# An expert layer's key products over two experts at once, with matching blocks kept, and one output product per half-tiled slot tile

## What is computed

```python
x = conv_attention(x)                 # q, k, v by 1x1 convolutions, softmax over rows of the image
t = tokens(x)                         # (4, 1024, 256)
t = t + mix(layer_norm(t))            # h W1 + (band h) W2 + bias
t = t + experts(layer_norm(t))

# experts: 32 of them, each with keys 256 x 64 and values 64 x 256
sel = sigmoid(xt @ expert_sel.T)      # (4096, 32)
sel_val, sel_idx = top_k(sel, 2)      # each token goes to two experts, weighted
h = relu(einsum('td,edh->teh', xt, keys))
out = einsum('teh,te,ehv->tv', h, w, values)   # w: zero but for the two chosen
```

## Time and profile before

| | |
|---|---|
| median of 3 runs | 510.26 us (509.55 to 510.54) |
| the profiled execution | 509.37 us |
| its span, first to last instruction | 507.6 us |
| granted TensorE clock, mean | 0.878 |
| instructions | 10650 |

### The profile page before, as it was taken

The page is one execution under the profiler, slowest core; times in us unless marked ns, Lnnn a source line. Parts: engine busy times, 40 slices in busy tenths (PEclk is TensorE's granted clock), DMA queues, the critical chain, the costliest instruction groups (busy, mean ns, idle before and its releaser), DMA issues.

```text
span 507.6 us, 10650 instructions
## 1 busy us (share of the span) xinstructions
PE 399.3 (79%) x3207; PEld 292.9 (58%) x3207; DVE 362.7 (71%) x1080; ACT 229.5 (45%) x604; POOL 321.6 (63%) x479
## 2 busy tenths in 40 slices
PE   8899999999999999999999885748676277766000
PEld 4677777877778877777676662336454154534000
DVE  3778999999999999999999667546454454556100
ACT  2214454544555454545454343339655556735000
POOL 5345558888778888688888777144555554636610
PEclk9899999999999999999999976879877768767555
DMA  8996001411111111121110012575554443431096
GB/s 202 330 213 182 11 23 54 126 53 44 53 33 47 49 54 44 44 52 45 54 52 35 22 63 74 134 234 156 164 153 133 124 135 109 123 95 50 3 206 125
DMA packets 28441, 49.55 MB, mean 98 GB/s; under 512 B 6204, under 2 KB 21966, under 8 KB 27373
## 3 DMA queue, kind: packets, MB, share of 16 engines
q1 hardware_dynamic: 20512, 26.69, 20.6%
q0 software_dynamic: 7872, 22.19, 14.1%
HBM read 30.74 MB, written 25.73 MB: 111 GB/s over the span
## 4 chain that ended last, share of the span: by engine, by line
PE 51%; issue 14%; DVE 13%; SPq 9%; POOL 3%; DMA 2%; another core or an unknown queue 1%; ACT 1%; DVEq 0%; POOLq 0%; ACTq 0%
PE bank L1189 17%; SPq L396 8%; PE bank L1129 6%; PE bank L1070 6%; PE E L1094 5%; PE bank L1243 3%; PE bank L1049 2%; PE E L1229 2%; PE bank L1162 2%; PE bank L1257 2%; DVE gmax L744 2%; POOL out L568 2%; PE bank L1170 2%; DVE gsum L792 2%; PE bank L1149 2%
## 5 line engine op out<-in xcount | busy, mean ns | idle before, releaser
L568 POOL DMA_INDIRECT out<-vT,dest x80 | 78.8, 985 | 68.7 <-DVE vT L1003 47.9
L1189 PE MATMUL bank<-vT,prob 128*128 128x256 f32 x512 | 118.8, 385 | 0.0
L1189 PEld LDWEIGHTS bank<-vT,prob 128*128 128x128 f32 x512 | 95.7, 191 | 12.2
L490 POOL TENSOR_TENSOR prob<-prob,ginv 128x1024 f32<-128x1024 f32 x32 | 61.0, 1907 | 28.1 <-DVE ginv L807 25.6
L472 POOL DMA_INDIRECT slot_rows<-rows,slot x64 | 68.4, 1069 | 12.7 <-issue 12.7
L990 DVE TENSOR_SCALAR q_s<-bank 128x256 f32<-128x256 f32 x20 | 8.5, 424 | 63.1 <-remote 56.1
L1257 PE MATMUL bank<-rows,q_s 64*64 64x256 f32 (+1 forms) x224 | 36.2, 479 | 19.2 <-DVE q_s L990 10.8
L665 ACT ACTIVATE prob<-E 128x512 f32<-128x512 f32 x40 | 22.7, 593 | 55.2 <-PE E L1229 34.5
L628 ACT ACTIVATE prob<-prob 128x1024 f32<-128x1024 f32 x32 | 33.8, 1057 | 20.8 <-DVE prob L748 20.8
L1243 PE MATMUL bank<-prob,k_s 128*64 128x64 f32 (+1 forms) x448 | 32.1, 297 | 13.9 <-issue 13.2
L1229 PE MATMUL E<-ident,xc_or_xin 128*128 128x128 f32 x160 | 28.9, 336 | 16.7 <-DMA xc_or_xin<-slot_rows 15.6
(11 more groups left out here) (200 smaller groups left out, 856.7 us busy)
## 6 DMA issues: line engine op xcount, KB each, us to landing
xc_or_xin<-slot_rows SPq DMA_DIRECT2D x48, 130.0 KB
xc_or_xin<-slot_rows SPq DMA_DIRECT2D x64, 65.0 KB
xt<-x_tok SPq DMA_DIRECT2D x32, 128.0 KB, 2.4
values_s<-values SPq DMA_DIRECT2D x2, 2048.0 KB, 28.3
out<-out POOLq DMA_DIRECT2D x4, 1024.0 KB, 14.1
xc_or_xin<-x_cm SPq DMA_DIRECT2D x3, 1024.0 KB, 20.3
keys_s<-keys SPq DMA_DIRECT2D x1, 2048.0 KB, 14.2
out<-vT,dest POOLq DMA_INDIRECT x80
```

The costliest lines, as they stand in the source:

```text
L490: g.tensor_tensor(prob[:, t % 2], prob[:, t % 2], ginv[:, t % 2].unsqueeze(2).to_broadcast([P, WT * KB, W]), ALU.mult).then_inc(prob_done, 1)
L568: g.indirect_dma_start(out=out, out_offset=bass.IndirectOffsetOnAxis(ap=dest[:, n % (2 * NB), k:k + 1], axis=0), in_=yb[:, n % NB, k, :], ...
L1189: mm = m.matmul(av_p, pr[:, j, :], vT[:, b % 2, j, :], start=(j == 0), stop=(j == KB - 1))
```

## The change

It changes the shapes of three products in the expert stage and what goes with them.

- Whole tiles, hidden: the keys of two tiles' experts stand side by side as 128 columns (`kk_two`), and one product takes them against the tokens of both tiles (256 columns). Of its result the blocks where keys and tokens belong together are kept (`H_two[side, :, r, :]`), the other two are not read. 4 products (8 records) of 128 columns with 256 token columns in place of 8 (16 records) of 64 with 128.
- Half tiles, hidden: the same with the two experts of one tile (`kk_half`): 8 products (16 records) of 128 columns with 128 token columns in place of 16 (32 records) of 64 with 64.
- Half tiles, outputs: the relu's results are put on the diagonal blocks of a buffer `hT_half` whose other blocks hold zeros, so one product of 128 x 128 with 256 columns does a tile: 4 (8 records) in place of 8 (16 records).
- The relu is two instructions, one for each half of the partitions, in every group; TensorE waits for both.
- GpSimd fills the zero blocks of `hT_half` (in a part of `t2` that is free by then) by two instructions behind the last scatter of token rows, and TensorE waits for them once, ahead of the first outputs of half tiles.
- Keys and values are copied in the same number of instructions of the same size to other places.

```diff
@@ GpSimd, behind the scatters of token rows
+            pool.wait_ge(u2_copied, 2 * GROUP * P // C)
+            for r in range(2):
+                g.memset(hT_half[r * HID:(r + 1) * HID, :, :, (1 - r) * HALF:(2 - r) * HALF], 0.0).then_inc(zeroed, 1)
@@ ScalarE, keys_copied
-                        done = a.activation(kk[:, n % 2, k, r], keys_s[:, :, bass.ds(expert[2 * k + r], 1), :].rearrange(
+                        into = kk_two[:, n % 2, k // 2] if parts(n) == 1 else kk_half[:, n % 2, k]
+                        done = a.activation(into[:, :, side_of(k if parts(n) == 1 else r)], keys_s[:, :, bass.ds(expert[2 * k + r], 1), :].rearrange(
@@ VectorE, hidden
-                v.tensor_scalar(hT[:, n % 2], H_p[n % 2], 0.0, None, ALU.max).then_inc(hid_out, 1)
+                for r in range(2):
+                    side = side_of(r)
+                    if parts(n) == 1:
+                        v.tensor_scalar(hT[side, n % 2], H_two[n % 2][side, :, r, :], 0.0, None, ALU.max).then_inc(hid_out, 1)
+                    else:
+                        tokens = slice(r * HALF, (r + 1) * HALF)
+                        v.tensor_scalar(hT_half[side, n % 2, :, tokens], H_half[n % 2][side, :, tokens], 0.0, None,
+                                        ALU.max).then_inc(hid_out, 1)
@@ TensorE, hidden
-                width = P // parts(n)
-                for two in range(GROUP // 2):
-                    for r in range(parts(n)):
-                        tokens = slice(r * width, (r + 1) * width)
+                if parts(n) == 1:
+                    for two in range(GROUP // 2):
+                        pair = slice(2 * two, 2 * two + 2)
                         for a in range(CH):
-                            for k in (2 * two, 2 * two + 1):
-                                mm = m.matmul(H_p[n % 2][side_of(k), two, tokens], kk[:, n % 2, k, r, a, :],
-                                              uT[:, n % 2, k, a, tokens], start=(a == 0), stop=(a == CH - 1))
+                            mm = m.matmul(H_two[n % 2][:, two], kk_two[:, n % 2, two, a, :], uT[:, n % 2, pair, a, :],
+                                          start=(a == 0), stop=(a == CH - 1))
+                else:
+                    for k in range(GROUP):
+                        for a in range(CH):
+                            mm = m.matmul(H_half[n % 2][:, k], kk_half[:, n % 2, k, a, :], uT[:, n % 2, k, a, :],
+                                          start=(a == 0), stop=(a == CH - 1))
@@ TensorE, outputs
-                width = P // parts(n)
-                for two in range(GROUP // 2):
-                    for r in range(parts(n)):
-                        tokens = slice(r * width, (r + 1) * width)
-                        for k in (2 * two, 2 * two + 1):
-                            mm = m.matmul(Y_p[n % 2][k % 2][tokens, two, :], hT[side_of(k), n % 2, two, tokens],
-                                          vv[side_of(k), n % 2, two, r, :], start=True, stop=True)
+                if n == WHOLE_GROUPS:
+                    pe.wait_ge(zeroed, 2)
+                for k in range(GROUP):
+                    h, w = ((hT[side_of(k), n % 2, k // 2], vv[side_of(k), n % 2, k // 2, 0, :]) if parts(n) == 1
+                            else (hT_half[:, n % 2, k], vv_half[:, n % 2, k, :]))
+                    mm = m.matmul(Y_p[n % 2][k % 2][:, k // 2, :], h, w, start=True, stop=True)
```

More of the change, by code:

```diff
@@ L193, in attention_moe @@
         uT = prob.rearrange("p b j v -> p b (j v)").rearrange("p b (k a n) -> p b k a n", k=GROUP, a=CH)
-        kk = k_s.rearrange("p b g j v -> p b (g j v)").rearrange("p b (k r a n) -> p b k r a n", k=GROUP, r=2, a=CH)
+        kk = k_s.rearrange("p b g j v -> p b (g j v)")
+        kk_two = kk[:, :, 0:GROUP * CH * HID].rearrange("p b (w a n) -> p b w a n", w=GROUP // 2, a=CH)
+        kk_half = kk.rearrange("p b (k a n) -> p b k a n", k=GROUP, a=CH)
         hT = q_s[:, 0].rearrange("p t w h -> p (t w h)").rearrange("p (b k n) -> p b k n", b=2, k=GROUP // 2)
@@ L198, in attention_moe @@
             "p (b k r n) -> p b k r n", b=2, k=GROUP // 2, r=2)
+        hT_half = t2[:, 0:2 * GROUP * P // C].rearrange("p t n -> p (t n)").rearrange("p (b k n) -> p b k n", b=2, k=GROUP)
+        vv_half = vv.rearrange("p b k r n -> p (b k r) n").rearrange("p (b k) n -> p b k n", k=GROUP)
         yb = vT[:, :, :, :].rearrange("p a (b k) n -> p (a b) k n", k=GROUP)
@@ L220, in attention_moe @@
         T_p = [E[:, q * 512:(q + 1) * 512].rearrange("p (k a n) -> p k a n", k=2, a=CH) for q in range(2)]
-        H_p = [bank[2 + b][:, 0:2 * P].rearrange("p (k n) -> p k n", k=GROUP // 2) for b in range(2)]
+        H_two = [bank[2 + b][:, :].rearrange("p (w k n) -> p w k n", w=GROUP // 2, k=2) for b in range(2)]
+        H_half = [bank[2 + b][:, :].rearrange("p (k n) -> p k n", k=GROUP) for b in range(2)]
         Y_p = [[bank[i + side][:, :].rearrange("p (k n) -> p k n", k=GROUP // 2) for side in range(2)] for i in (6, 4)]
@@ L251, in attention_moe @@
         coef_done, rebuilt = sem("coef_done"), sem("rebuilt")
+        zeroed = sem("zeroed")
         cols_out, T_mm, T_out, H_mm, hid_out = sem("cols_out"), sem("T_mm"), sem("T_out"), sem("H_mm"), sem("hid_out")
@@ L1014, in values_copied @@
                     for r in range(parts(n)):
-                        done = v.tensor_copy(vv[side_of(k), n % 2, k // 2, r, :],
-                                             values_s[side_of(k), bass.ds(expert[2 * k + r], 1), :].rearrange(
-                                                 "p e n -> p (e n)"))
+                        side = side_of(k if parts(n) == 1 else r)
+                        into = vv[side, n % 2, k // 2, 0, :] if parts(n) == 1 else vv_half[side, n % 2, k, :]
+                        done = v.tensor_copy(into, values_s[side, bass.ds(expert[2 * k + r], 1), :].rearrange("p e n -> p (e n)"))
                 done.then_inc(values_out, 1)
@@ L1235, in hidden @@
                 if n >= 2:
[L1236 to L1244 removed]
+                    pe.wait_ge(hid_out, 2 * (n - 1))
+                if parts(n) == 1:
+                    for two in range(GROUP // 2):
+                        pair = slice(2 * two, 2 * two + 2)
+                        for a in range(CH):
+                            mm = m.matmul(H_two[n % 2][:, two], kk_two[:, n % 2, two, a, :], uT[:, n % 2, pair, a, :],
[5 more added lines that the diff above has]
+                                          start=(a == 0), stop=(a == CH - 1))
                 mm.then_inc(H_mm, 1)
             def outputs(n):
[L1248 removed]
+                pe.wait_ge(hid_out, 2 * n + 2)
                 pe.wait_ge(values_out, n + 1)
```

## The result

The changed kernel takes 504.21 us (median of 20 runs), the kernel before 508.56 us beside it (20 runs): a ratio of 0.9919, 95% interval 0.9895 to 0.9943, so 0.8% faster. The profiled execution of the changed kernel has a span of 503.6 us, against 507.6 before.

A forecast was written before the change was run, and what follows sets the result against it. It took the expert stage as a loop from release to release, held by scattered rows in flight. Relu 14 x 0.38 = 5.3 us, all else 0, on 509.37 gives 514.7, plus 0.9 for the median: 515.6; range 505 to 527.

The forecast's parts named there:

- The relu: VectorE's L990 split in two: 0.38 us more in each of 14 bursts, 5.3 us (4.8 to 6.4).
- The products' own time: TensorE's hidden products and half-tile outputs take longer: 12 x 0.83 + 8 x 1.6 = 23 us at full clock.
- The products' price of 0: TensorE's added work lies in the 8 to 13 us between releases, where it stands still 5 us: costed at nothing.
- the reading of a release: Expert stage: while scattered rows are in flight, TensorE's reports arrive late or not; the last row's landing releases everything.
- The prediction's 1.47: Expert stage: the release comes 1.47 us after the eighth scatter of a burst ends, part of the 13.42 us cycle.
- Rival B: Expert stage: TensorE's crawl of one instruction each 0.7 us sets the release, so fewer matmuls shorten it: 504; chance 0.17.
- TensorE drains at a change of shape: On TensorE, each change of shape costs 0.1 to 0.15 us; 36 fewer save 5 us; part of B and C.
- Rival A: TensorE late in half-tile groups, or whole-tile bursts of eight split: 11 to 13 us on top, 527; chance 0.23.
- Rival C: Expert stage: the loop waits for SyncE's loads, not the scatters; relu costs nothing, no change, 510.5; chance 0.14.

The follow-up runs named there:

- relu2: The kernel before with only the relu split into two instructions of 64 partitions: 512.03 us, ratio 1.0068 to the kernel before.
- wide_many: The changed kernel with its products cut in two, giving the matmul counts of before at the new width: 513.36 us, ratio 1.0122 to the kernel before.
- tiny_again: The changed kernel with eight one-column matmuls ahead of the hidden products of every whole-tile group, on a third chip: 512.42 us, ratio 1.0029 to the kernel before.
- no_rows: The kernel before with scatters issued but a bound that drops nearly all their rows: 508.20 us, ratio 0.9999 to the kernel before.
- one_of_four: The kernel before with only the last of each group's four scatters issued: 462.32 us, ratio 0.9081 to the kernel before.
- half_only: The kernel before with the change in the 8 groups of half tiles alone: 509.76 us, ratio 1.0006 to the kernel before.
- third set: Runs on a third chip: kernel before (510.88 us), changed kernel (507.15 us, ratio 0.9924), early3_again and tiny_again.
- early3: The kernel before with the change in groups 0 to 2 alone, on the chip where the kernel before takes 470.46 us: 470.60 us, ratio 0.9998.
- early3_again: The kernel before with the change in groups 0 to 2 alone, repeated on a third chip: 507.49 us, ratio 0.9949 to the kernel before.

## Why the prediction was wrong

**The relu.** Right in kind, too dear by a third: 3.5 us against 5.3 (bounds 4.8 to 6.4). By the traces the stretch from relu 0 to relu 11 grew by 2.6 us, about what 0.38 for each of the six or seven relus on its chain gives; the one from there to relu 19, with a relu on the chain in each of eight groups, grew by 1.9 where the same rate gives 3.0. (These are single executions, and relu2's reached its first relu 1.7 us sooner than that of before.)

**The products' own time.** Right for each: L1259 takes 1.99 us in a whole-tile group (1.92 predicted) and 3.75 at the lower clock. Their sum was not: TensorE is busy 100.9 us from 322 to 465 instead of 95.2, 5.6 more where the prediction had 23, because the products before were already stretched, by jams and by a lower clock (granted 0.78 there, 0.87 after). A change with the old counts, wide_many, cost 1.2%, about 6 us; the forecast's sum was 5.3. That is near by luck in part: the relu, all that was in that sum, cost 3.5.

**The products' price of 0: the step that failed.** The prediction said that TensorE's work lies in the 8 to 13 us between releases and so has no effect, "no gain comes of it". It asked what the products need of the engine, and not what their number does to the report that VectorE waits for. In the whole tiles wide_many and tiny_again hold the engine's time, or nearly (0.34 us a group more), and double the number of matmuls in the hidden product: they are 2.0% and 1.1% slower than the changed kernel (ratios 1.0122 and 1.0029 against 0.9919 and 0.9924). The gain of 0.8% and the 0.7% of the relus that it covered, 1.5% together, lie between the two.

**Behind it, the reading of a release.** "While scattered rows are in flight" was taken from two ends that coincided, and no_rows refutes it. One_of_four shows the cause to be the issuing of the scatters by GpSimd (or something that goes with their number, such as packets and reports; these were not told apart). The row that should have raised doubt was in hand: L568 has 0.98 us each in all states, and in before every release comes 0.9 to 1.9 us after the last scatter of a burst has ended, never within the burst. (The prediction's 1.47 holds for the two releases it read; 390.86 comes 1.63 after, 404.71 1.91.) The Trainium skill, "Perfetto Trace Analysis", section "DMA Instruction — SWDGE (GPSIMD)", says that such an instruction's interval in a profile is the generation of descriptors and not the movement of data. This case agrees: with rows or without them the scatter lasts 0.98 us.

**Rival B** had the direction, the place and a time of 504. Its mechanism was TensorE's crawl of one instruction per 0.7 us, and its sign came true: products end amid the scatters of a burst and their reports pass at once (at 334.03 and 349.25; relus at 334.28 and 349.37). Of its prices, "issue" fell by 15.0 us where it had 8.6, the relu's "remote" by 24 us between 345 and 500 (51.0 to 26.8), and 4 to 5 us of all that reached the end. My argument against it, that the release also reaches VectorE, whose matmuls were through 8 us earlier, was none: VectorE waits for TensorE's report, and the report is what is late. B's sum counted both kinds of groups, and half_only shows that the half tiles give nothing that can be measured. That TensorE drains at a change of shape is not the cause: wide_many has the changed kernel's shapes, with as few changes between them, and no gain. **Rival A** had one of its signs, more than 14 waits, but not its price: GpSimd waited 16 times for 44.5 us instead of 14 times for 47.9, the pauses over a microsecond part the scatters into 13 bursts and not 14, and where a burst came near to splitting, the pause is 0.85 us (scatter at 353.34). **Rival C** had the loads as the bound. It can't be set aside for the half tiles. Its sign, half-tile groups that keep their time although the relu is longer, is there in the first pair of traces (61.9 and 61.7 us from relu 11 to relu 19) and not in the third set's (61.6 and 63.2). TensorE's wait for rows grew by 11 us from 322 to 470 (15.6 to 27.0), again by 11 in the third set (21.2 to 32.5), and is 27.5 in half_only. And on the page's chain of work that ended last, SyncE's issuing of half-tile loads is the largest part of the expert stage, 8% of the span before (L396) and 7% after (L402). So it may be that there the loads, slowed by the same jams, take what the products give; no run changed the loads, and this is argued and not shown.

Open: why a report passes in the midst of scatters in one group and not in the next, whether the instructions ahead of the report or those behind it count (tiny_again has them ahead, wide_many on both sides), why halving the count gains nothing in the half tiles, and why one chip has no jams.

## What to carry to other kernels

When an engine waits for "remote" and the work it waits for ended long ago, the number of instructions on the reporting engine can be part of the price, beside their time (here in the whole tiles; in the half tiles half the number gained nothing): restore the count at no engine time (tiny matmuls) to measure it. Judge a wait by what is issued around it and take the issuing and the traffic away separately, before tying it to one of them. And a gain of this kind is the cover of a larger fault: fewer indirect scatters are worth up to 45 us of this kernel's 508 where the jams are (an upper bound, as one_of_four leaves out three quarters of the output; the chip without jams is 38 us faster with all of them), the change 4.

## What the runs showed of the hardware

The same kernel takes 470.5 us on one chip and 507.7 to 511 on the others, and the difference is the stage with indirect scatters: from the first relu to the last 99.6 us in early3 there, 135.7 in early3_again here. Where the jams are, SyncE and TensorE step by 0.66 to 0.80 us per instruction while GpSimd issues scatters back to back (64 and 25 such steps in the kernel before), the increment of a semaphore can be recorded 5.9 to 8.6 us after the end of the product that makes it, and dropping the scatters' bytes (22.1% to 2.0% of the DMA engines) changes neither. Eight matmuls of one column, 0.34 us of TensorE per group, cost 5.3 us in twelve groups.
